# Attention kernel: where the biases are added, and one turn of the output moved to the next step

## What is computed

```python
Q = split_heads(x @ Wq.T + bq)
K = split_heads(x @ Wk.T + bk)
V = split_heads(x @ Wv.T + bv)
scores = jnp.einsum('bhqd,bhkd->bhqk', Q, K) / math.sqrt(hd)
scores = scores + prior_lambda * _gaussian_mask(Lx)[None, None, :, :]
attn = jax.nn.softmax(scores, axis=-1)
out = jnp.einsum('bhqk,bhkd->bhqd', attn, V)
...
return out @ Wo.T + bo
...
x = x + 0.5 * _L0_ffn_ref(_layernorm(x, axis=-1), ...)
x = x + _L0_attn_ref(_layernorm(x, axis=-1), ...)
x = x + 0.5 * _L0_ffn_ref(_layernorm(x, axis=-1), ...)
```

## Time and profile before

| what | value |
| --- | --- |
| median of the runs | 986.99 us (lowest 986.05) |
| profiled execution: time | 986.02 us |
| profiled execution: span, first to last instruction | 984.2 us |
| busy, share of the span | PE 92%, PEld (weight load) 66%, DVE 75%, ACT 60%, POOL 58% |
| mean granted TensorE clock | 0.967 of full speed |
| from one `kq_hi` copy to the next, inside a run of turns | 26 such intervals; 21 of them 16.52 to 16.69 us, the others 16.30, 16.31, 16.38, 17.01 and 17.15 us |

### The profile page before, as it was taken

The page is one execution under the profiler, slowest core; times in us unless marked ns, Lnnn a source line. Parts: engine busy times, 40 slices in busy tenths (PEclk is TensorE's granted clock), DMA queues, the critical chain, the costliest instruction groups (busy, mean ns, idle before and its releaser), DMA issues.

```text
span 984.2 us, 33646 instructions
## 1 busy us (share of the span) xinstructions
PE 905.6 (92%) x12732; PEld 650.2 (66%) x12732; DVE 741.1 (75%) x2092; ACT 588.2 (60%) x1108; POOL 573.1 (58%) x658
## 2 busy tenths in 40 slices
PE   7688889789999999999999999999999999998993
PEld 6587645479755555556995555557985557955993
DVE  6858489772599999999657999998329987576454
ACT  3434666545677666666557777665567775575631
POOL 4572777730157566655104777774256777775775
PEclk8799879989999999999999999999999999999997
DMA  8815557265334332224552222325662228924755
GB/s 256 258 45 125 155 149 219 62 130 129 115 110 144 113 102 78 66 73 90 130 138 78 75 83 69 88 70 126 160 171 62 86 72 152 212 88 77 187 124 138
DMA packets 203580, 118.19 MB, mean 120 GB/s; under 512 B 98560, under 2 KB 194399, under 8 KB 203296
## 3 DMA queue, kind: packets, MB, share of 16 engines
q1 hardware_dynamic: 188320, 89.40, 34.1%
q0 software_dynamic: 15104, 26.65, 10.9%
HBM read 35.07 MB, written 64.26 MB: 101 GB/s over the span
## 4 chain that ended last, share of the span: by engine, by line
PE 74%; DVE 9%; issue 7%; ACT 3%; SPq 2%; DMA 2%; POOL 2%; ACTq 0%; POOLq 0%; DVEq 0%
PE banks L613 17%; PE banks L749 11%; PE banks L778 8%; PE banks L724 7%; PE banks L572 4%; PE banks L574 4%; PE banks L573 4%; DVE row_max L1627 3%; ACT probs L1035 2%; PE banks L716 2%; PE banks L518 2%; PE banks L789 2%; PE banks L857 2%; DVE kq_lo L1667 2%; PE banks L845 1%
## 5 line engine op out<-in xcount | busy, mean ns | idle before, releaser
L1627 DVE TENSOR_REDUCE row_max<-banks 128x2 f32<-128x512 f32 x512 | 338.9, 684 | 77.2 <-PE banks L749 74.1
L1035 ACT ACTIVATE probs<-banks 128x512 f32<-128x512 f32 x512 | 278.0, 595 | 133.2 <-PE banks L749 133.1
L1136 POOL DMA_INDIRECT big<-yg,slots x236 | 228.6, 969 | 196.7 <-issue 105.9
L1122 POOL DMA_INDIRECT xg<-xs,slots x236 | 236.2, 1001 | 112.1 <-issue 75.9
L613 PE MATMUL banks<-w_all,h_f 128*128 (+1 forms) x1600 | 211.7, 277 | 1.9 <-DVE x_all L1492 1.9
L613 PEld LDWEIGHTS banks<-w_all,h_f 128*128 128x128 f32 x1600 | 195.7, 194 | 4.9 <-issue 2.3
L943 ACT ACTIVATE h_f<-banks 128x512 f32<-128x512 f32 x200 | 119.4, 597 | 132.2 <-PE banks L574 128.6
L778 PE MATMUL banks<-probs,v_op 128*32 128x256 f32 x2048 | 168.0, 383 | 0.6 <-ACT probs L1035 0.6
L749 PE MATMUL banks<-band_parts,thirds 96*32 96x296 bf16 (+2 forms) x4096 | 167.0, 276 | 0.0
L724 PE MATMUL banks<-q_op,k_op 32*128 32x256 bf16 x1024 | 121.6, 275 | 16.7 <-issue 6.9
L749 PEld LDWEIGHTS banks<-band_parts,thirds 96*32 96x32 bf16 x4096 | 94.7, 95 | 56.3 <-issue 56.3
(11 more groups left out here) (176 smaller groups left out, 1271.8 us busy)
## 6 DMA issues: line engine op xcount, KB each, us to landing
yg<-y_rows SPq DMA_DIRECT2D x77, 256.0 KB
q_in<-kq_kept SPq DMA_DIRECT2D x96, 64.0 KB
k_op<-kq_kept SPq DMA_DIRECT2D x96, 64.0 KB
xg<-zeros SPq DMA_DIRECT2D x5, 896.0 KB
kq_kept<-kq_hi SPq DMA_DIRECT2D x32, 128.0 KB
kq_kept<-kq_lo SPq DMA_DIRECT2D x32, 128.0 KB
xg<-zeros SPq DMA_DIRECT2D x1, 3968.0 KB
xg<-zeros SPq DMA_DIRECT2D x2, 1984.0 KB
```

The lines of the kernel that those rows point to most:

```text
L1035: act.activation(probs[:, four % 2, u % 4, :], banks[:, ST[u % 2], :], ACT.Exp).then_inc(A["exp_done"], 1)
L1122: pool.indirect_dma_start(xg[q], bass.IndirectOffsetOnAxis(slots[:, q % 4, c, t:t + 1], 0), xs[:, NTH[q] % 2, t, :], None, bounds_check=CA ...
L1136: pool.indirect_dma_start(y_back[:, i, c, :], None, yg[q], bass.IndirectOffsetOnAxis(slots[:, q % 4, c, t:t + 1], 0)).then_inc(gathered[i] ...
L1627: dve.tensor_reduce(row_max[:, gp, :, qt, j], banks[:, MX[(16 * b + v) % 3], :].rearrange("p (k c) -> p k c", k=2), AX.X, ALU.max).then_in ...
```

## The change

1. The bias of queries and keys leaves PE: two products per sequence go. The biases are loaded as columns (`bias_cols`, one value per partition) in place of broadcast rows. ACT adds it when it makes `kq_hi` (two activations of 256 columns with a bias operand, in place of one of 512), and DVE when it makes `kq_lo` (two operations of 256 columns with a per-partition scalar, in place of one of 512).
2. The output bias is one product of 256 columns in place of two of 128.
3. `o_n` is turned in step 6, between the prior and `weighted`, not at the end of step 5. ACT's copy to `o_t` moves from behind exponential 11 to behind exponential 12, ahead of 13.
4. `bias_parts` and its constants shrink from 384 to 128 columns.

```diff
-            sp.dma_start(bias_rows[:, 0, :], bq.broadcast_to([P, D])).then_inc(attn_in, 16)
-            sp.dma_start(bias_rows[:, 1, :], bk.broadcast_to([P, D])).then_inc(attn_in, 16)
+            sp.dma_start(bias_cols[:, 0:1], bq.rearrange("o d -> d o")).then_inc(attn_in, 16)
+            sp.dma_start(bias_cols[:, 1:2], bk.rearrange("o d -> d o")).then_inc(attn_in, 16)
...
@@ project (PE)
                     pe.matmul(o, w_hi[:], a_xt_hi[:], start=True, stop=False)
                     pe.matmul(o, w_hi[:], a_xt_lo[:], start=False, stop=False)
-                    pe.matmul(o.rearrange("p (t c) -> p t c", t=KT), bias_parts[:, which, :], bc(three_rows[:], 1, KT),
-                              start=False, stop=False)
                     mm = pe.matmul(o, w_lo[:], a_xt_hi[:], start=False, stop=True)
...
@@ turn (PE)
                     if s == 5:
                         if main:
                             weighted(b, par, 3)
+                    if s == 6:
                         if behind:
                             wait(pe, A["o_ready"], b)
                             for t in range(KT):
...
                             wait(pe, A["x_added"], b - 1)
+                            pe.matmul(banks[:, M[0], 0:KT * D].rearrange("p (t c) -> p t c", t=KT), three_rows[:],
+                                      bc(bias_parts[:], 1, KT), start=True, stop=False, skip_group_check=True)
                             for t in range(KT):
-                                o = banks[:, M[0], bass.ts(t, P)]
-                                pe.matmul(o, three_rows[:], bias_parts[:, 2, :], start=True, stop=False)
-                                mm = pe.matmul(o, o_t[:, bass.ts(t, P)], wstage[:, 3, :], start=False, stop=True)
+                                mm = pe.matmul(banks[:, M[0], bass.ts(t, P)], o_t[:, bass.ts(t, P)], wstage[:, 3, :],
+                                               start=False, stop=True, skip_group_check=True)
                             mm.then_inc(A["proj_done"], 1)
...
@@ high_part (ACT)
-                act.activation(kq_hi[:].rearrange("p w c -> p (w c)"), banks[:, MB(b), :],
-                               ACT.Copy).then_inc(A["kq_hi_ready"], 1)
+                if b == 0:
+                    act.wait_ge(bias_ready, 1)
+                act.activation(kq_hi[:, 0, :], banks[:, MB(b), 0:L], ACT.Identity, bias=bias_cols[:, 0:1], scale=1.0)
+                act.activation(kq_hi[:, 1, :], banks[:, MB(b), L:2 * L], ACT.Identity, bias=bias_cols[:, 1:2],
+                               scale=1.0).then_inc(A["kq_hi_ready"], 1)
...
@@ turn (ACT), behind each exponential u
+                        if u == 12 and behind:
+                            wait(act, A["on_turned"], b)
+                            wait(act, A["proj_done"], b - 1)
+                            act.activation(o_t[:], banks[:, M[1], 0:L], ACT.Copy).then_inc(A["o_ready2"], 1)
...
-                    if s == 5 and behind:
-                        wait(act, A["on_turned"], b)
-                        wait(act, A["proj_done"], b - 1)
-                        act.activation(o_t[:], banks[:, M[1], 0:L], ACT.Copy).then_inc(A["o_ready2"], 1)
...
@@ low_part_of (DVE)
-                dve.tensor_tensor(kq_lo[:].rearrange("p w c -> p (w c)"), banks[:, MB(b), :],
-                                  kq_hi[:].rearrange("p w c -> p (w c)"), ALU.subtract).then_inc(A["kq_ready"], 1)
+                dve.scalar_tensor_tensor(kq_lo[:, 0, :], banks[:, MB(b), 0:L], bias_cols[:, 0:1], kq_hi[:, 0, :],
+                                         ALU.add, ALU.subtract)
+                dve.scalar_tensor_tensor(kq_lo[:, 1, :], banks[:, MB(b), L:2 * L], bias_cols[:, 1:2], kq_hi[:, 1, :],
+                                         ALU.add, ALU.subtract).then_inc(A["kq_ready"], 1)
```

More of the change, by code:

```diff
@@ L266, in build @@
         wv_lo = sb("wv_lo", [P, P], BF16)
-        bias_rows = sb("bias_rows", [P, 3, D])
+        bias_rows = sb("bias_rows", [P, D])
+        bias_cols = sb("bias_cols", [P, 2])
         k_rows = sb("k_rows", [P, 2])
@@ L295, in build @@
         o_t = sb("o_t", [P, L])
-        bias_parts = sb("bias_parts", [P, 3, D], BF16)
+        bias_parts = sb("bias_parts", [P, D], BF16)
         three_rows = sb("three_rows", [P, P], BF16)
@@ L377, in _ @@
                 sp.dma_start(wstage[:, n, :], w).then_inc(attn_in, 16)
-            sp.dma_start(bias_rows[:, 0, :], bq.broadcast_to([P, D])).then_inc(attn_in, 16)
-            sp.dma_start(bias_rows[:, 1, :], bk.broadcast_to([P, D])).then_inc(attn_in, 16)
+            sp.dma_start(bias_cols[:, 0:1], bq.rearrange("o d -> d o")).then_inc(attn_in, 16)
+            sp.dma_start(bias_cols[:, 1:2], bk.rearrange("o d -> d o")).then_inc(attn_in, 16)
             sp.dma_start(bv_b[:], bv.broadcast_to([P, D])).then_inc(attn_in, 16)
-            sp.dma_start(bias_rows[:, 2, :], bo.broadcast_to([P, D])).then_inc(attn_in, 16)
+            sp.dma_start(bias_rows[:], bo.broadcast_to([P, D])).then_inc(attn_in, 16)
             sp.dma_start(lam_b[:], lam.broadcast_to([P, 1])).then_inc(attn_in, 16)
@@ L1594, in bias_constants @@
                 dve.memset(three_rows[:], 0.0)
-                done(dve.tensor_scalar(bias_rows[:, 0, :], bias_rows[:, 0, :], QSCALE, None, ALU.mult))
+                done(dve.tensor_scalar(bias_cols[:, 0:1], bias_cols[:, 0:1], QSCALE, None, ALU.mult))
                 done(dve.tensor_copy(bias_parts[:], bias_rows[:]))
```

## The result

The changed kernel takes 997.72 us against 986.99 us: a ratio of 1.0109 (95% interval 1.0086 to 1.0132). It is slower by about 11 us; 995 was forecast. On each side one execution of four took far longer (2066.44 us before, 1624.56 us changed), and the ratio is of the other three. The profiled execution took 997.98 us, with a span of 996.2 us against 984.2.

What follows compares the result with a forecast made beforehand. Bound: a loop of PE and DVE works and waits, 16.53 us a turn. Growth of 0.33 over 29 turns (9.6), two later turns (0.7) and setup (-1.5) give +8.8 on 986.02: 995 us, range 990 to 999 (8 in 10: 982 to 1002).

Steps and rivals of the forecast that it cites:

- Maximum 4, and not `o_n`, holds PE at step 6: Step 6's fourth group of scores waits for DVE's maximum 4, so removing step 5's wait for `o_n` wins nothing.
- A: The piece of a turn from step 4's scores to step 6's prior, 4.50 us before, forecast to become 4.69.
- The rival that step 5 was PE's bound: Step 5's wait for `o_n` and its 0.37 us would really go: turn 16.27 us, time 978 us, chance 0.12.
- `kq_lo` in two operations, +0.19: DVE's two operations, on the loop ahead of maximum 4, take 0.79 against 0.60 us: +0.19 us a turn.
- `kq_hi` at 0: ACT's two activations in place of one take longer but hide at either end, with no table load: priced at 0.
- The turn's price in step 6, +0.37: Turning `o_n` between prior and `weighted`, where PE is alone on the loop, costs its whole 0.37 us a turn.
- One output bias product, -0.01: In step 6, one product of 256 columns takes 0.11 us against two of about 0.06: -0.01 us a turn.
- Bias products in `project`, -0.22: Two of eight go, each 0.10 to 0.11 us of PE's issue just ahead of step 4: -0.22 us a turn.
- PE idle about 1 us at step 6 for a maximum: A sign in the new profile: this idle time replaces PE's wait for `o_n`.
- The copy to `o_t` in time by 0.05: In step 6, ACT's copy is usable at +1.33 and PE ready at +1.38 us after the prior: 0.05 to spare.
- the slow rival: The copy to `o_t` comes late and PE waits in step 6: turn grows 0.71 us, time 1006.5 us, chance 0.08.
- Setup, -1.5: Ahead of the turns, smaller DVE constants save about 1.1 us and four bias products fewer 0.4.

Runs made afterwards that it cites:

- e1: Changed kernel with the turn of `o_n` back in step 5 and ACT's copy to `o_t` back behind exponential 11: 982.28 us, ratio 0.9967.
- e3: Changed kernel with `kq_lo` in one operation of 512 columns again, leaving its bias out: ratio 1.0056 to the kernel before.
- e4: Changed kernel with `kq_hi` in one activation of 512 columns again, leaving its bias out: 998.71 us, ratio 1.0144.
- e2: Kernel before with only the turn of `o_n` moved to step 6 and ACT's copy behind exponential 12: 1.58% slower.
- e9: Changed kernel with the turn of `o_n` back in step 5, and step 6's output product between the prior and `weighted`: ratio 0.9983.
- e11: Kernel before with only the output bias as one product of 256 columns: ratio 0.9964.
- e10: Changed kernel with DVE's `rden` and `o_n` moved from step 4 to step 5, between maxima 4 and 5: 979.30 us.
- e13: Kernel before, old biases, with the turn of `o_n` in step 6 and `rden` and `o_n` in step 5: no measurable difference, 16.60 us a turn.
- e6: Kernel before with only `kq_lo` moved from step 4 to step 5, between maxima 4 and 5: 16.24 us a turn, with single turns longer.
- e5: Changed kernel with the turn of `o_n` back in step 5 and `kq_lo` moved to step 5: 16.29 us a turn, with single turns longer.
- e12: Kernel before with `kq_lo` in step 5, output bias in one product, and `kq_hi`'s transfers issued early: 982.65 us, ratio 0.9940.

## Why the prediction was right, and where it was off

- **Maximum 4, and not `o_n`, holds PE at step 6.** Right. With the turn of `o_n` gone from step 5 nothing was won there (A 4.68 in the changed kernel and in e1), and the wait moved to the maxima as foretold. The rival that step 5 was PE's bound is out.
- **`kq_lo` in two operations, +0.19.** Right to the hundredth (e3). The row with the same operands was the right one to choose.
- **`kq_hi` at 0.** Right (e4). ACT's table loads are 12 in the kernel before and 12 in the changed one, 1.28 us each, so the new operands brought none.
- **The turn's price in step 6, +0.37.** This is the term that was mis-sized: it is +0.50 (e1, e2). I took the transposes' length from where they follow other products, and the 0.42 to the next group from where that group is the weighted products. e9 shows the missing 0.14 as a price of the place.
- **One output bias product, -0.01.** It is -0.11 (e11). I priced the columns alone; the rows show that the float32 products behind it became shorter together, 0.54 us (410.48 to 411.02) against 0.66 (0.77 less the two bias products' 0.11).
- **Bias products in `project`, -0.22.** It is -0.17. The other 0.05 is at the end of the projection: its last product is followed by step 4's scores after 0.27 us (403.90 to 404.17), and after 0.20 before (401.43 to 401.63). Why that distance grew was not tried.
- Together the turn grew by 0.41 instead of 0.33 us: +0.13 - 0.10 + 0.05. So the sum is closer than its terms, because two of the errors offset each other; that is luck. By 0.41 a turn, 28 turns would add 11.5 us; it was 10.55, partly because behind turn 16 some turns of the kernel before take 16.60 to 16.69 us, where those of the changed one stay at 16.93.
- **PE idle about 1 us at step 6 for a maximum.** The 1.0 us is there, but 0.4 of it is a wait for exponential 11.
- **The copy to `o_t` in time by 0.05.** Right; the slow rival is out.
- **Setup, -1.5.** PE's projection starts 1.9 us earlier, and turn 1 only 1.0. Neither proves the term: each is of one execution, and turn 1's `rden` starts anywhere from 149.6 to 157.8 us in the profiles of the experiments.
- **The phase ahead of turn 30** grew by 2.45 us (66.32 against 63.87), where I had only one turn's growth. There PE is idle for 2.33 us ahead of the first feed-forward product, and the granted clock is 0.50 in the 2.5 us behind it (829.00 to 831.50). The moved turn is not enough for it: the same phase takes 64.0 us in e3 and 64.6 in e2, which have the move too, 65.1 in e4, and 66.4 in e1, which does not have it. Why that product starts so late there (its data come by transfers that SP issued at the same distance behind `kq_lo` as before) was not tried and is open; each number is of one execution.

## What to carry to other kernels

Where two engines are both over 90% busy, write down the loop from one point of the period to the same point of the next, and price an edit by the piece of the loop it stands in: here a step taken out of a visible wait gave nothing, because the next wait stood right behind it, and cost 0.50 us in its new place. Such a move can pay only if what it waited for is moved with it, and then only if that piece gives back more than the new place costs: with the new biases 0.62 us against 0.51 (e10 against e1), with the old ones 0.43 against 0.51, which wins nothing (e13). And when a producer is moved later, follow it to its transfers: 1.9 us later was too late for them in single turns.

## What the runs showed of the hardware

- A full-width product between two groups of 32-wide ones costs about 0.14 us more than behind them (it starts 0.57 to 0.58 us behind the prior's products, in the changed kernel and e9, where a 32-wide group starts 0.42 behind them).
- One bf16 bias product of 256 columns ahead of two float32 products takes 0.11 us less than two of 128 columns that alternate with them.
- The waits of up to 0.5 us inside the turns left PE's granted clock at 1.00 (in the changed kernel PE is idle for 0.34 us and PEld for 0.53 ahead of the scores at 408.53, and the clock is 1.00 from 400.00 to 420.00). Some of the longer ones were followed by stretches at 0.50 to 0.70: those of 2.11 us (e6), 2.33 (changed kernel) and 1.64 (e5). Others were not: 2.18 us (e12) and 1.63 (e6). So the length of a wait alone does not tell here whether the clock falls. The stretches (PE, PEld, DVE, ACT, POOL, clock, DMA) of the changed kernel, of e5 and of e12, behind their waits:

```profile
829.00:831.50 2.50, 2.39 (x18) 1.45 (x18) 0.47 (x2) 0.60 (x1) 0.74 (x1) 0.50 1.11 209
```

```profile
313.40:316.40 3.00, 3.00 (x38) 1.79 (x39) 0.76 (x2) 1.46 (x3) 1.40 (x2) 0.52 0.52 133
```

```profile
455.00:458.00 3.00, 2.44 (x25) 1.36 (x26) 1.85 (x6) 1.11 (x2) 0.58 (x1) 1.00 0.55 102
```
